# Spreading 1/sum by a DMA through DRAM, two groups' PV outputs in one bank, and PV runs of 11 tiles

## The reference

```python
x = L0_attn_x                                     # (1, 2048, 128)
sa, ca, ga, sb, cb, gb = modulation from silu(c) @ wmod   # ga, gb with |.| at least 0.25
h = _layernorm(x) * (1 + ca) + sa
qkv = einsum('bse,ehd->bshd', h, w_qkv)           # 16 heads, 64 wide
logits = einsum('bqhd,bkhd->bhqk', q, k) / 8      # causal mask
probs = softmax(logits)
out = einsum('bhqk,bkhd->bqhd', probs, v)
x = x + ga * einsum('bshd,hde->bse', out, w_out)
h = _layernorm(x) * (1 + cb) + sb
x = x + gb * ffn(h)      # 8 experts of 128 -> 512 -> 128, one chosen for each token by argmax
```

## Time and profile before

| | us |
|---|---|
| median of 3 runs | 1068.56 (1068.03 to 1071.42) |
| the profiled execution, its own time | 1070.3 |
| its span, first to last instruction | 1068.6 |
| PE busy | 999.0 |
| ACT busy | 718.1 |
| DVE busy | 695.2 |

### The profile page before, as it was taken

The page is one execution under the profiler, slowest core; times in us unless marked ns, Lnnn a source line. Parts: engine busy times, 40 slices in busy tenths (PEclk is TensorE's granted clock), DMA queues, the critical chain, the costliest instruction groups (busy, mean ns, idle before and its releaser), DMA issues.

```text
span 1068.6 us, 20055 instructions
## 1 busy us (share of the span) xinstructions
PE 999.0 (93%) x7293; PEld 764.7 (72%) x7293; DVE 695.2 (65%) x2197; ACT 718.1 (67%) x1323; POOL 44.0 (4%) x60
## 2 busy tenths in 40 slices
PE   3999999999999999999999999999999999985494
PEld 2677777777777777777777777777777777764494
DVE  4876667765866487666785586657766678655244
ACT  2877767767777677776776666767777677642372
POOL 1000000000000000000000000000000000003442
PEclk9999999999999999999999999999999999996697
DMA  9400020002100020002000110002000100020223
GB/s 215 70 21 1 21 50 21 2 3 49 40 1 2 20 51 21 1 21 51 21 1 20 37 35 1 2 20 51 21 1 21 40 21 1 2 99 19 57 65 111
DMA packets 39981, 34.86 MB, mean 33 GB/s; under 512 B 13224, under 2 KB 28880, under 8 KB 39888
## 3 DMA queue, kind: packets, MB, share of 16 engines
q1 hardware_dynamic: 38480, 31.00, 12.3%
q0 software_dynamic: 1408, 2.63, 0.7%
HBM read 11.25 MB, written 5.60 MB: 16 GB/s over the span
## 4 chain that ended last, share of the span: by engine, by line
PE 88%; DVE 4%; DMA 3%; issue 2%; POOL 1%; ACT 1%; SPq 0%; DVEq 0%; POOLq 0%; ACTq 0%
PE ps L659 25%; PE ps L696 23%; PE ps L670 21%; PE ps L638 5%; PE ps L679 3%; PE ps L707 3%; PE ps L642 2%; PE ps L776 2%; PE ps L784 2%; DMA k_split<-k_split 1%; POOL x_sorted L593 1%; DVE q_split L967 1%; PE ps L747 1%; ACT q_split L832 1%; DMA probs<-in_L_wmod_dram 0%
## 5 line engine op out<-in xcount | busy, mean ns | idle before, releaser
L659 PE MATMUL ps<-k_split,q_split 128*128 128x512 f32 (+2 forms) x1280 | 371.1, 398 | 5.6 <-DMA k_split<-k_split 3.6
L846 ACT ACTIVATE probs<-probs,neg_max 128x128 f32<-128x128 f32 (+15 forms) x256 | 308.5, 1206 | 42.8 <-DVE neg_max L995 40.6
L988 DVE TENSOR_SCALAR_CACHE_REDUCE probs<-ps 128x512 f32<-128x512 f32 (+1 forms) x384 | 249.6, 668 | 100.7 <-PE ps L670 66.7
L854 ACT COPY pT<-ps 128x512 f32<-128x512 f32 (+1 forms) x435 | 234.1, 563 | 111.0 <-PE ps L670 106.8
L670 PE MATMUL ps<-ident,probs 128*128 128x128 f32 x2176 | 304.6, 273 | 1.3 <-DVE pT L1007 1.3
L670 PEld LDWEIGHTS ps<-ident,probs 128*128 128x128 f32 x2176 | 256.5, 141 | 60.5 <-issue 29.6
L696 PE MATMUL ps<-pT,v_sb 128*64 128x256 f32 (+1 forms) x2304 | 272.6, 373 | 0.0
L659 PEld LDWEIGHTS ps<-k_split,q_split 128*128 128x128 f32 x1280 | 202.0, 190 | 49.5 <-issue 28.9
L696 PEld LDWEIGHTS ps<-pT,v_sb 128*64 128x64 f32 x2304 | 152.2, 136 | 87.0 <-issue 26.6
L991 DVE CUSTOM_DVE_ANT_0 probs<-ps,causal 128x256 f32<-128x256 f32 (+3 forms) x256 | 130.9, 512 | 28.8 <-PE ps L659 27.7
L1007 DVE COPY pT<-ps 128x512 f32<-128x512 f32 (+1 forms) x141 | 92.4, 659 | 32.7 <-PE ps L670 30.4
(11 more groups left out here) (125 smaller groups left out, 608.0 us busy)
## 6 DMA issues: line engine op xcount, KB each, us to landing
k_split<-k_split SPq DMA_DIRECT2D x64, 256.0 KB, 3.7
probs<-in_L_ffn_W_dram SPq DMA_DIRECT2D x1, 2048.0 KB, 8.4
hT<-x_sorted SPq DMA_DIRECT2D x29, 64.5 KB, 1.8
x_sorted<-zeros SPq DMA_DIRECT2D x1, 1856.0 KB, 14.8
w_pair<-in_L_attn_w_qkv_dram SPq DMA_DIRECT2D x24, 64.0 KB, 3.4
x_sb<-in_L_attn_x_dram SPq DMA_DIRECT2D x4, 256.0 KB, 5.5
accT<-y_rows SPq DMA_DIRECT2D x4, 256.0 KB, 3.7
out_dram<-accT SPq DMA_DIRECT2D x4, 256.0 KB, 2.8
```

Source lines behind the costliest of these rows:

```text
L659: m = pe.matmul(ps_ring[:, s.bank, 0:w], q_split[r % 2][:, q0:q0 + P], k_split[r % 2][:, part, k0:k0 + w], start=(part == 0), stop=(part = ...
L846: act.activation(row, row, ACT.Exp, bias=neg_max[:, g, r:r + 1], accum_out=row_sum[:, g, r:r + 1]).then_inc(exp_done, 1)
L854: act.copy(pT[:, n % PT_SLOTS, lo:BANK], ps_turn[:, n % TURN_BANKS, lo:BANK]).then_inc(turn_taken[n % TURN_BANKS], 1)
L988: dve.tensor_scalar(row, ps_ring[:, bank, 0:w], 1.0, LOWEST, ALU.mult, ALU.max, accum_out=highest).then_inc(bank_free[bank], 1)
```

## The change

Three things are changed together in the attention.

**1/sum by DMA.** `bcast` and `spread` are gone, from PE and ACT. SP now stores the 512 reciprocals of a group into a row of a DRAM tensor (`put`, 4-byte elements, L554 of the changed kernel) and reads the row back over the 64 partitions of each head (`get`, two DMAs, L565) into `rinv_b`, which is twice as wide. A `get` waits for its `put` to have landed. `norm` waits for the four `get`s of a part on a semaphore.

**Two groups in one bank.** The pv of group 2c writes columns 0 to 255 of `ps_o`, that of 2c+1 columns 256 to 511. One `norm` of 512 columns follows the two (32 instead of 64), and only the first pv of an even group waits for the norm before.

**The planner.** `PV_BATCH` is 11, and the rule that starts a run at 3 tiles is gone; `SCORE_TILES` limits the lead of scores over turns a second way; the biases of `take` are other ones. SP's order comes from the plan too (`transfers`). Two small tables for the sorting are made by GpSimd after the last pv, in room that the attention used.

```diff
-PV_BATCH = 6
+PV_BATCH = 11
 SCORE_LEAD = 1.4
+SCORE_TILES = 24.0
+TAKE_ACT = -1500.0
+TAKE_DVE = 600.0
+ADD_DVE = 1000.0
...
-    BIAS = dict(act=dict(take=-800.0), dve=dict(take=300.0, add=2000.0))
+    BIAS = dict(act=dict(take=TAKE_ACT), dve=dict(take=TAKE_DVE, add=ADD_DVE))
...
-            past = group_before(p, g) if key[2] == 0 else None
-            return max(at("take", *key), at("value", p, key[2] // 4), at("norm", *past) if past else 0.0)
+            past = group_before(p, g) if key[2] == 0 and g % 2 == 0 else None
+            return max(at("take", *key), at("value", p, key[2] // 4), at("norm", past[0], past[1] // 2) if past else 0.0)
...
-        order = [("bcast", in_pv or pv_past), ("pv", in_pv), ("proj", due <= PROJ_LEAD),
-                 ("pv", waiting >= PV_BATCH or (whole and waiting >= min(PV_BATCH, 3))),
-                 ("out", True), ("back", True), ("score", score_at - turn_at < SCORE_LEAD), ("turn", True),
-                 ("score", True), ("pv", True), ("proj", due <= PROJ_LEAD + 2), ("bcast", True)]
+        early = score_at - turn_at < SCORE_LEAD and self.tiles_to(score_at) - self.tiles_to(turn_at) < SCORE_TILES
+        order = [("pv", self.mode == "pv"), ("proj", due <= PROJ_LEAD), ("pv", waiting >= PV_BATCH),
+                 ("out", True), ("back", True), ("score", early), ("turn", True), ("score", True), ("pv", True),
+                 ("proj", due <= PROJ_LEAD + 2)]
...
+                elif s.kind == "put":
+                    g = s.key[1]
+                    n = p * GROUPS + g
+                    sp.wait_ge(rinv_ready, n + 1)
+                    sp.dma_start(spread_rows[n].rearrange("(u h) i -> i u h", h=2),
+                                 rinv[:, g, :].rearrange("p (u h) -> p u h", h=2),
+                                 allow_slow_non_contiguous=True).then_inc(spread_put[n % PUTS], 16)
+                elif s.kind == "get":
+                    g = s.key[1]
+                    n, part = p * GROUPS + g, p * NC + g // 2
+                    sp.wait_ge(spread_put[n % PUTS], 16 * (n // PUTS) + 16)
+                    if part >= 2:
+
+                        sp.wait_ge(o_ready, part - 1)
+                    for h in range(2):
+                        sp.dma_start(rinv_b[own_half(h), part % 2, QG * (g % 2):QG * (g % 2) + QG
+                                            ].rearrange("p (u i) -> p u i", u=2),
+                                     spread_rows[n:n + 1, h::2, :].broadcast_to([D, 2, P])
+                                     ).then_inc(spread_in[part % 2], 16)
...
-                elif s.kind == "bcast":
-                    pe.wait_ge(rinv_ready, p * GROUPS + g + 1)
-                    if s.use:
-                        pe.wait_ge(bank_free[s.bank], s.use)
-                    for u in range(2):
-                        for h in range(2):
-                            m = pe.matmul(ps_ring[D * h:D * h + D, s.bank, P * u:P * u + P],
-                                          rinv[:, g, 2 * u + h:2 * u + h + 1].to_broadcast([P, D]), ident[:],
-                                          start=True, stop=True, skip_group_check=True)
-                    m.then_inc(bank_full[s.bank], 1)
...
-                        m = pe.matmul(ps_o[D * h:D * h + D, P * u0:QG], v_sb[:, j, D * h:D * h + D],
+                        m = pe.matmul(ps_o[D * h:D * h + D, o_half + P * u0:o_half + QG], v_sb[:, j, D * h:D * h + D],
...
-                    act.copy(rinv_b[:, g % 2, :], ps_ring[:, bank, 0:QG]).then_inc(bank_free[bank], 1)
...
-                    dve.tensor_tensor(oT[:, g * QG:(g + 1) * QG], ps_o[:, 0:QG], rinv_b[:, g % 2, :],
+                    dve.tensor_tensor(oT[:, c * BANK:(c + 1) * BANK], ps_o[:], rinv_b[:, part % 2, :],
                                       ALU.mult).then_inc(o_ready, 1)
```

More of the change, by code:

```diff
@@ L35 @@
 DOUBLING = 3600.0
+PUT = 2400.0
+GET = 2600.0
+PUTS = 4
 NEVER = 1e18
@@ L66 @@
 class Plan:
-    IN_RING = ("score", "bcast", "out", "proj", "back")
-    EMPTIES = {"top": "score", "lo": "proj", "value": "proj", "spread": "bcast", "add": "out", "resid": "back"}
+    IN_RING = ("score", "out", "proj", "back")
+    EMPTIES = {"top": "score", "lo": "proj", "value": "proj", "add": "out", "resid": "back"}
     def __init__(self):
@@ L81, in __init__ @@
         ends = [(PAIRS - 1, c) for c in range(CHUNKS)]
-        keys = dict(score=scores, turn=turns, pv=turns, bcast=groups, out=parts,
+        keys = dict(score=scores, turn=turns, pv=turns, out=parts,
                     proj=[(p, c, j) for p, c in parts for j in range(3)], back=ends,
                     top=scores, exp=[(p, g, r) for p, g in groups for r in range(4)], take=turns,
-                    hi=splits, lo=splits, value=parts, sum=groups, spread=groups, norm=groups,
+                    hi=splits, lo=splits, value=parts, sum=groups, norm=parts,
                     add=parts, resid=ends)
@@ L111, in __init__ @@
         self.span = max(clock.values())
+        self.sp = self.transfers()
         self.ring_uses = [len(range(b, len(self.uses), RING)) for b in range(RING)]
[L114 to L115 removed]
+    KINDS = dict(pe=("score", "turn", "pv", "out", "proj", "back"),
+                 act=("hi", "value", "take", "exp"),
                  dve=("norm", "sum", "lo", "add", "resid", "top", "take"))
[L117 to L118 removed]
+    FIRST = dict(act=("hi", "value"), dve=("sum", "norm", "lo"))
+    BIAS = dict(act=dict(take=TAKE_ACT), dve=dict(take=TAKE_DVE, add=ADD_DVE))
     def at(self, kind, *key):
@@ L171, in ready, with get_from, got, transfers @@
         return at({"hi": "proj", "lo": "hi", "add": "out", "resid": "back"}[kind], *key)
+    def get_from(self, p, g):
+        before = p * CHUNKS + g // 2 - 2
+        free = self.at("norm", before // CHUNKS, before % CHUNKS) if before >= 0 else 0.0
+        return max(self.at("sum", p, g) + PUT, free)
+    def got(self, p, g):
+        return self.get_from(p, g) + GET
+    def transfers(self):
+        steps = []
+        for p in range(PAIRS):
+            for c in range(CHUNKS):
+                steps.append((self.at("lo", p, c, 1), "keys", (p, c)))
+            for g in range(GROUPS):
+                steps.append((self.at("sum", p, g), "put", (p, g)))
+                steps.append((self.get_from(p, g), "get", (p, g)))
+            if p + 1 < PAIRS:
+                steps.append((self.at("lo", p, 1, 1) + HOP, "qkv_weights", (p + 1,)))
+                steps.append((max(self.at("lo", p, 2, 1), self.at("out", p - 1, CHUNKS - 1) if p else 0.0) + HOP,
+                              "out_weights", (p + 1,)))
+        order = [Step(kind, key, 0, 0) for _, kind, key in sorted(steps)]
+        begun = [0, 0]
+        for s in order:
+            if s.kind in ("put", "get"):
+                begun[s.kind == "get"] += 1
+                assert begun[0] - begun[1] <= PUTS
+        return order
     def bank_of(self, kind, *key):
@@ L180, in took @@
         if engine == "pe":
-            columns = self.mode in ("pv", "bcast")
-            if kind == "bcast":
-                return 440.0 + (0.0 if columns else 142.0)
+            columns = self.mode == "pv"
             if kind == "pv":
```

113 lines of the change are left out of this document (57 added, 56 removed).

## The result

The changed kernel is slower: 1098.01 us median (1094.0 to 1101.4, 4 runs) against 1068.4, ratio 1.027 with a 95% interval of 1.0247 to 1.0292. The forecast was 1021.5 and its range ended at 1037.

The account below looks back on a forecast made before the run. The prediction took PE, full from its own instructions, to bound the attention. It summed 30 + 17 − 0.4 = 47 us, so 1068.6 − 47 = 1021.5; own range 1015 to 1028, range of 8 in 10 1014 to 1037.

Parts of the forecast that it names:

- what bounds the kernel: Attention: PE is full from its own instructions, so work leaving its queue shortens the span while other engines keep up.
- part 1: PE's queue in the attention: 64 bcasts leave, at 0.44 to 0.49 us each, taken as 30 us saved.
- Part 3: DVE: 64 norms become 32 of twice the width, 0.69 us each; costs 0 to 0.4 us once, at the end.
- part 2: PE: 128 stays in column mode (stretches of pv and bcast) become 68, at 0.28 us each, 17 us saved.
- the time that the order allows: From a group's reciprocals to its pv's end: some 8.9 us for a pair's first part, a margin of 1.4 us.
- part 4: Way through DRAM, reciprocal to norm: chain of 7.5 us, bounds 5.7 to 22.4, costing nothing in the forecast.
- the price of being late: Norm of each pair's first part: each us late costs 1 us per pair, eight times; about 15 us of chain eats the 47.
- New waits: PE waits 0.2 to 0.5 us after each of 68 long pv runs, 14 to 34 us back: 1028 to 1055; chance 0.14.
- Very late: Norm of a pair's first part waits on a chain of 18 to 22.4 us: 1110 to 1178; chance 0.04 for 1072 or more.
- A little late: Norm of each pair's first part 2 us late with an 11 us chain, 16 us lost: 1037; chance 0.07.

Follow-up runs that it names:

- e5: Changed kernel, but 1/sum spread by bcast matmuls on PE and ScalarE's copy as before, no DMA in the norm's way: 1044.92 us, ratio 0.977.
- e6: e1 with PV_BATCH 6 in place of 11, so 107 stays in column mode instead of 68: 1036.49 us, ratio 0.969.
- e9: Changed kernel, norm not waiting for gets and multiplying by a tile of x; put of 256 4-byte elements side by side: 1023.7 us, put lands in 7.8.
- e11: Changed kernel, norm not waiting for gets, which read x; put of 512 4-byte elements 64 bytes apart: 1015.7 us, put lands in 2.2.
- e1: Changed kernel without puts and gets, rinv_b filled with 1, outputs not divided by the sums; also called the floor: 1014.12 us, ratio 0.948.
- e4: Changed kernel in its own order, put storing 256 elements of 8 bytes in place of 512 of 4: 1026.28 us, ratio 0.960.
- e7: e4 with the planner told 4.5 us for the put and 4.7 for the gets: 1017.4 us, ratio 0.951.
- e3: Changed kernel with the planner told 9.5 us for the put and 5.5 for the gets, nothing else changed: 1032.59 us, ratio 0.964.

## Why the prediction was wrong, step by step

**Right: what bounds the kernel, and about right the size of part 1.** PE was the bound, and 64 bcasts were worth 30.8 us by the medians (26.6 by the profiled executions), taken as 30 with 28.2 to 31.4 as bounds. Part 3 was right too: the norm of 512 columns takes 0.692 us for the 0.69 taken, and the 0.8 us of idle time at the end are as small as forecast.

**Right in kind, too small: part 2.** It was taken as 17 us with 20.4 as its upper end, and e5 shows 23.8 to 27.7. Of that, 4.8 us are small idle times of PE, seen in the earlier trace rows and not in e5, which the step didn't count. The other 22.9 are busy time, 0.38 for a stay, and e6 has 0.45, so a price from a few rows of full runs was too low; why was not measured beyond the waits in e6. The Trainium skill (TensorE: Matmul & The Clock Gate, section Step-by-step: what each phase is for) gives about 128 cycles for the drain behind a matmul, and the estimate from it, 6.4 us in all, is far below what both runs show. Parts 1 and 2 together were forecast at 47 and measured at 54.6 (1068.7 to 1014.1).

**Right for seven pairs: the time that the order allows.** It was counted as 8.9 us for the first part; the trace has 9.2 to 9.9 in the second to eighth pair. In the first pair of all it is 4.8, so even the forecast's own chain of 7.5 us would have been 2.7 us late there. The pieces in the earlier trace rows that the step starts from are group 3 of one pair and then group 1 of the next; the text read them rightly.

**Wrong: part 4, the length of the chain.** The step took 7.5 us, and it was 14.9:

- the put was taken as 4.5 us, on a line by number of elements between 128 loaded into SBUF and 3712 stored, and was 8.1, and 9.2 in the pair shown. e9 and e11 show that the line was wrong as such: side by side, the count matters little, and the neighbourhood much. Neither of its ends was a row of the same kind. The row of 2.7 us was a read from DRAM and said nothing on a store into it. The 19.4 us were a store of 4-byte elements, but into one column of `x_sorted`, whose rows are 129 floats long, so its elements stand 516 bytes apart: 5.2 ns for each, near to the 4.3 of e11 and not to the 15.8 of the put (estimates, time to landing by the number of elements).
- the gets were taken as 3.0 us and took 4.4, issue of both included.
- SP was said to add nothing, and added 1.3 us, as the put stood behind a copy of keys. In the first pair it is worse: the put of group 1 stands 6.5 us behind the gets of group 0, which wait for their own put, and PE stops for 12.6 us. No run issues the puts from another queue, so what SP's order alone costs was not measured.

The bounds were given as 5.7 to 22.4, and 14.9 lies within; the chance of 4% for a chain of 15 or more did not follow from those bounds but from the belief in the line. With a margin of 1.4 us and an unknown that could be 15 us longer, the chances had to be far nearer to each other. The forecast's text even had the point at which it turns, 15 us.

**Wrong: the price of being late.** It was put at 1 us for each us late, once in each pair, which for 14.9 would have made a kernel as fast as before. Measured: 57.7 us of idle time in front of `out` and 84 us in all over the floor. Of the 57.7, some 49 are the stops of the eight first parts, 12.6 of them in the first pair; some 7.5 are shorter stops in later parts, which had been given a margin of 8 us or more, and 0.8 is the end of the attention. Most of the rest is the clock of PE, which the forecast let stay: 22.8 us more busy time for the same instructions. It stood at 0.50 (the level of 1.2 GHz) around the end of the stops shown, and the mean over the span was 0.948 against 0.976.

**The rivals.** "New waits" from long runs did not come: in e1 PE is idle for 3 us in the whole attention. "Very late" was the right mechanism at the right place, and had the chance of 4%. Its prices leave out the clock as well. "A little late" is the same mechanism with a chain of 11 us.

## What to carry to other kernels

When work moves from a full engine to a chain of DMAs, compare the chain's length with the time that the order allows at its tightest place, and price it by a row of the same kind: a store by a store, with the same elements side by side. An order written by a planner is worth what its table of durations is worth: telling it the true 9 or 15 us in place of 5 gave back 9 us (e4 to e7) and 65 us (e3). And if the margin at the tightest place is smaller than what is unknown of the chain, the forecast has two likely outcomes, not one.

## What the runs showed of the hardware

- Stores of 4-byte elements side by side in DRAM land in 7.8 to 9.5 us for 256 or 512 of them; the same 512 elements 64 bytes apart land in 2.2, and 128 elements of 16 bytes, the same 2 KB side by side, in 2.1. The Trainium skill (DMA: Bandwidth & Descriptors, section Specifications) says that transfers below 512 bytes become a read and a write of what is there; the elements of all these shapes are below that, and their times differ by a factor of about four, so the rule alone does not tell a good small store from a bad one.
- Around stops of PE of 4.7 to 12.6 us its granted clock was 0.50, and stayed so for 3 to 6 us after PE started again, while a stop of 1.1 us left by e4 left the out after it at its full speed. A stop of 3.65 us in e4 was followed by slow instructions, a turn at 0.72 us from start to start:

```profile
54.41 1.42 PE L757 MATMUL ps<-oT,wo_pair 128*128 128x512 f32 x2 [3.65 <-DVE probs L1032]
55.62 1.06 PE L729 MATMUL ps<-ident,probs 128*128 128x128 f32 x4
56.34 2.06 PE L718 MATMUL ps<-k_split,q_split 128*128 128x512 f32 x4
...
379.62 1.10 PE L757 MATMUL ps<-oT,wo_pair 128*128 128x512 f32 x2 [1.14 <-issue]
```
